# Seven shared PSUM banks and a two-key-tile order in a fused decoder layer on one core

## What is computed

```python
x = x + attn(layernorm(x))            # causal self-attention, 2 heads of 64, rotary positions
x = x + xattn(layernorm(x), ctx)      # 16 heads of 8 over 1601 context rows
x = x + ffn(layernorm(x))             # 128 -> 512 -> 128, erf-GELU, weights with a
                                      # correction taken from 16 of the tokens
# xattn, per batch b and head h:
scores = einsum('bhqd,bhkd->bhqk', Q, K) / sqrt(8)
ctx    = einsum('bhqk,bhkd->bhqd', softmax(scores), V)      # then @ Wo + bo
```

## Time and profile before

| | |
|---|---|
| median of three runs | 377.39 us |
| the profiled execution | 377.22 us |
| its span in the trace | 375.4 us |
| TensorE busy, share of the span | 350.0 us, 93% |
| VectorE busy | 297.1 us, 79% |
| ScalarE busy | 296.4 us, 79% |
| GpSimd busy | 123.5 us, 33% |
| mean granted TensorE clock | 0.986 |

### The profile page before, as it was taken

One profiled execution on the slowest core, in us unless ns is written; L12 is line 12 of the kernel. 1 busy time (PEld: TensorE's weight loads), 2 busy tenths in 40 slices (PEclk: granted clock), 3 DMA queues, 4 the chain that ended last, 5 costly groups with the idle time before them and its releaser, 6 DMA issues.

```text
span 375.4 us, 11889 instructions
## 1 busy us (share of the span) xinstructions
PE 350.0 (93%) x4819; PEld 163.1 (43%) x4819; DVE 297.1 (79%) x601; ACT 296.4 (79%) x598; POOL 123.5 (33%) x202
## 2 busy tenths in 40 slices
PE   7778899999999999999999999999999999999996
PEld 3332343544545444444534445434433434443455
DVE  3779978699998997699999987999977879780013
ACT  1653258989898789898897898898987999799762
POOL 3510746398020205799310133382000036000000
PEclk9999988999999999999999999999998999999999
DMA  7535495033420221135302022023020101000001
GB/s 246 199 107 154 158 274 181 2 135 129 120 84 2 99 95 56 58 131 179 129 27 78 2 79 58 3 63 134 13 69 2 63 19 58 17 2 3 16 2 30
DMA packets 20010, 30.72 MB, mean 82 GB/s; under 512 B 1432, under 2 KB 17218, under 8 KB 19956
## 3 DMA queue, kind: packets, MB, share of 16 engines
q1 hardware_dynamic: 19956, 29.97, 24.8%
HBM read 18.62 MB, written 11.34 MB: 80 GB/s over the span
## 4 chain that ended last, share of the span: by engine, by line
PE 58%; DVE 20%; POOL 10%; ACT 8%; issue 4%; DMA 1%; DVEq 0%; ACTq 0%; POOLq 0%
PE wsum L1191 19%; DVE part_max L785 15%; PE score L1205 13%; PE ring L1161 12%; PE ring L1227 6%; ACT probs L1004 4%; POOL k_parts L630 3%; POOL k_rest L670 2%; POOL k_parts L675 2%; PE score L1161 1%; PE ring L1244 1%; ACT q_unit L1015 1%; PE ring L1252 1%; PE ring L1258 1%; POOL xn L686 1%
## 5 line engine op out<-in xcount | busy, mean ns | idle before, releaser
L785 DVE TENSOR_REDUCE part_max<-ring 128x1 f32<-128x512 f32 x384 | 239.0, 683 | 27.1 <-PE ring L1227 25.3
L1004 ACT ACTIVATE probs<-score 128x512 f32<-128x512 f32 (+1 forms) x416 | 223.3, 597 | 31.3 <-PE score L1205 28.4
L1191 PE MATMUL wsum<-probs,v_aug 128*32 128x256 f32 (+1 forms) x1664 | 134.6, 392 | 3.0 <-ACT unit_ctx L1009 2.9
L1205 PE MATMUL score<-q_unit,k_unit 51*128 51x256 bf16 (+1 forms) x832 | 128.7, 275 | 4.1 <-ACT probs L1004 3.5
L1227 PE MATMUL ring<-k_unit,q_unit 51*128 51x512 bf16 x384 | 121.3, 387 | 3.1 <-DVE part_max L785 2.1
L1205 PEld LDWEIGHTS score<-q_unit,k_unit 51*128 51x128 bf16 (+1 forms) x832 | 48.8, 96 | 97.9 <-ACT probs L1004 57.6
L1191 PEld LDWEIGHTS wsum<-probs,v_aug 128*32 128x32 f32 (+1 forms) x1664 | 39.3, 109 | 39.5 <-issue 20.2
L1227 PEld LDWEIGHTS ring<-k_unit,q_unit 51*128 51x128 bf16 x384 | 35.2, 94 | 17.4 <-DVE part_max L785 9.2
L630 POOL TENSOR_TENSOR max_parts<-neg_max,c_sb 128x8 bf16<-128x8 f32 x16 | 3.4, 210 | 111.9 <-DVE neg_max L793 111.9
L802 DVE RECIPROCAL unit_rsum<-ring 128x8 f32<-128x8 f32 x16 | 3.2, 201 | 21.6 <-PE ring L1252 21.6
L1015 ACT ACTIVATE q_unit<-ring 3x512 bf16<-3x512 bf16 x32 | 18.6, 580 | 1.1 <-PE ring L1244 0.8
(11 more groups left out here) (137 smaller groups left out, 337.8 us busy)
## 6 DMA issues: line engine op xcount, KB each, us to landing
k_unit<-k_rows SPq DMA_DIRECT2D x30, 300.2 KB
ctx_sb<-ctx_t SPq DMA_DIRECT2D x3, 800.5 KB, 8.6
k_rows<-k_parts SPq DMA_DIRECT2D x3, 601.5 KB, 3.2
k_rows<-k_parts SPq DMA_DIRECT2D x3, 599.2 KB, 3.3
even<-ffn_rows SPq DMA_DIRECT2D x3, 512.0 KB, 4.0
q_unit<-q_rows SPq DMA_DIRECT2D x30, 48.0 KB
k_rows<-k_parts SPq DMA_DIRECT2D x3, 401.0 KB, 4.1
k_rows<-k_parts SPq DMA_DIRECT2D x3, 399.5 KB, 3.9
```

Of the source, the lines that this page charges most:

```text
L785: v_.tensor_reduce(part_max[:, par, q, head, hp, c:c + 1], ring[s][:, 0:MW], AX.X, ALU.max)\
L1004: a_.activation(probs[0:rows, i % PB, :], score[k % EB][0:rows, :], ACT.Exp)\
L1191: last = mm(wsum[32 * j:32 * j + 32, 0:S], v_aug[0:rows, v // UB % 3, at:at + 32], probs[0:rows, i % PB, S * (j // 2):S * (j // 2 + 1)], s ...
L1205: last = mm(score[i % EB][0:keys, S * hp:S * (hp + 1)], k_unit[rows, u, L * hp + P * t:L * hp + P * t + keys], q_unit[rows, u, hp, :], sta ...
```

## The change

All seven banks beside `wsum` become one ring (`NR = 7`), which S items and the `HIDDEN` feed-forward steps also take from, in plan order. `wsum` is now where `keep` writes, and the two `keep` ahead of the last `norm` are gone. The `last` item becomes `l0` and `l1`, each with a slot of the ring.

The order inside a unit changes. PV items come in twos, behind every key tile with an odd running number `g = 13 v + t`. Side work of an even `g` (but for `t = 12`) is held and goes behind the odd key tile after it, ahead of that one's own side work. Where the two PV items belong to two units, the first one goes ahead of the side work and the second behind it. `COUNT`, `SIDE`, `TURN_AT` and the `HIDDEN` order stay.

```diff
-EB = 3
-NR = 4
+NR = 7
...
-TAIL = (("keep", 2), ("norm", UNITS - 1), ("keep", 2), ("post", "G0", 2), ("post", "OT", 3), ("keep", 4), ("post", "G1", 2),
+TAIL = (("norm", UNITS - 1), ("keep", 2), ("post", "G0", 2), ("post", "OT", 3), ("keep", 4), ("post", "G1", 2),
...
-        ("post", "last", 3))
+        ("post", "l0", 3), ("post", "l1", 3))
...
 def sums_due(v, t):
     g, h = KT * v + t, KT * HIDDEN_AT[0] + HIDDEN_AT[1]
-    due = range(g - 3, g) if g == h else () if g in (h + 1, h + 2) else range(g - 3, g - 2)
-    return [("PV", *divmod(i, KT)) for i in due if i >= 0]
+    due = range(g - 3, g) if g == h else range(g - 4, g - 2) if g % 2 else ()
+    return [("PV", *divmod(i, KT)) for i in due if i >= 0 and not (g > h > i)]
...
-    plan = []
+    plan, held = [], []
...
         plan += now
+        side = held
         if t == 4 and v:
-            plan.append(("norm", v - 1))
+            side.append(("norm", v - 1))
         if t == TURN_AT[u] and v + 1 < UNITS:
-            plan.append(("mT", v + 1))
+            side.append(("mT", v + 1))
         for *what, off in (SIDE if b < B - 1 else SIDE_LAST).get((u, t), []):
             if 0 <= b + off < B:
-                plan.append((*what, b + off))
+                side.append((*what, b + off))
         if (v, t) in VALUES_AT:
-            plan.append(("prep", VALUES_AT[v, t], 1))
+            side.append(("prep", VALUES_AT[v, t], 1))
         if (v, t) in OUT_AT:
-            plan.append(OUT_AT[v, t])
-        plan += sums
+            side.append(OUT_AT[v, t])
+        held = side if (KT * v + t) % 2 == 0 and t < KT - 1 else []
+        if len({item[1] for item in sums}) == 2:
+            plan.append(sums.pop(0))
+        plan += sums if held else side + sums
...
     for item in PLAN:                                   # ring_slots
-        if item in BANKS or item[0] not in ("M", "mT", "norm", "prep", "post") or item[1] in NO_SLOT:
+        if item[0] == "S":
+            if item[4]:
+                continue
+            item = item[:4]
+        elif item[0] not in ("M", "mT", "norm", "prep", "post") or item[1] in NO_SLOT:
             continue
...
             def exponential(item):
-                i, k = score_index(*item[1:4]), BANKS[item[:4]]
+                i, (s, n) = score_index(*item[1:4]), take(item[:4])
...
-                act.wait_ge(score_filled, k + 1)
-                a_.activation(probs[0:rows, i % PB, :], score[k % EB][0:rows, :], ACT.Exp)\
-                    .then_inc(score_drained, 1)
+                a_.activation(probs[0:rows, i % PB, :], ring[s][0:rows, :], ACT.Exp).then_inc(drained[s], 1)
...
             def keep(n):
-                    mm(score[0][:, :], still[:, 0:P], still[:, :], start=True, stop=True)
+                    mm(wsum[:, :], still[:, 0:P], still[:, :], start=True, stop=True)
...
             def scores(v, t, n, hp, par):
-                if hp == 0 and i >= EB:
-                    pe.wait_ge(score_drained, i - EB + 1)
-                last = mm(score[i % EB][0:keys, S * hp:S * (hp + 1)],
+                if hp == 0 and used:
+                    pe.wait_ge(drained[s], used)
+                last = mm(ring[s][0:keys, S * hp:S * (hp + 1)],
```

More of the change, by code:

```diff
@@ L234, in unit_plan @@
         plan += now
+        side = held
         if t == 4 and v:
-            plan.append(("norm", v - 1))
+            side.append(("norm", v - 1))
         if t == TURN_AT[u] and v + 1 < UNITS:
-            plan.append(("mT", v + 1))
+            side.append(("mT", v + 1))
         for *what, off in (SIDE if b < B - 1 else SIDE_LAST).get((u, t), []):
             if 0 <= b + off < B:
-                plan.append((*what, b + off))
+                side.append((*what, b + off))
         if (v, t) in VALUES_AT:
-            plan.append(("prep", VALUES_AT[v, t], 1))
+            side.append(("prep", VALUES_AT[v, t], 1))
         if (v, t) in OUT_AT:
-            plan.append(OUT_AT[v, t])
-        plan += sums
+            side.append(OUT_AT[v, t])
[3 more added lines that the diff above has]
+        plan += sums if held else side + sums
+    assert not held
     assert not todo
@@ L270 @@
 NO_SLOT = ("ln1", "ln2", "ln3", "soft", "store0", "store1", "split", "pn", "parts0", "parts1", "pa0", "pb0", "pa1", "pb1",
-           "stats", "low", "load", "G0", "G1", "last")
+           "stats", "low", "load", "G0", "G1")
 APART = {("prep", *item[1:]) for item in PLAN if item[0] == "ev"}
@@ L292, in ring_slots @@
     return slots
[L295 to L306, removed]
 RING = ring_slots()
@@ L421, in decoder_kernel @@
         ring = [ctx.enter_context(nc.psum_tensor(f"ring{i}", [P, 512], F32)) for i in range(NR)]
-        score = [ctx.enter_context(nc.psum_tensor(f"score{i}", [P, 512], F32)) for i in range(EB)]
         wsum = ctx.enter_context(nc.psum_tensor("wsum", [P, 512], F32))
@@ L479, in decoder_kernel @@
         low_done = sem("low_done")
-        last_sums = sem("last_sums")
-        last_y = sem("last_y")
         y_free = sem("y_free")
@@ L593, in _ @@
                         .then_inc(even_in, 16)
[L594 to L597, removed]
+                elif kind == "post" and item[1] in ("l0", "l1"):
+                    q = int(item[1][1])
+                    s, n = RING[item]
+                    sp.wait_ge(drained[s], n + 1)
+                    sp.dma_start(out[item[2], P * q:P * (q + 1), :], y_out[:, item[2] % 2, q, :]).then_inc(y_free, 16)
                 elif kind == "post" and item[1] == "out":
@@ L963, in post @@
                     last.then_inc(drained[s], 1)
-                elif name == "last":
+                elif name in ("l0", "l1"):
                     dve.wait_ge(y_free, 16 * (pb // 2 * 2 + 1))
                     dve.wait_ge(x2_b2_set, pb + 1)
[L967 to L970, removed]
+                    s, n = take(item)
+                    q = int(name[1])
+                    v_.tensor_tensor(y_out[:, pb % 2, q, :], ring[s][:, 0:D], x2_b2[:, pb % 3, q, :], ALU.add)\
+                        .then_inc(drained[s], 1)
                 elif name == "out":
@@ L1125, in post @@
                         .then_inc(drained[s], 1)
[L1126 to L1129, removed]
+                elif name in ("h0", "h1") and pb < 2:
+                    s, n = take(item)
+                    gelus(ring[s], pb, int(name[1])).then_inc(drained[s], 1)
                 elif name in ("G0", "G1"):
@@ L1179, in products @@
                 u = v % UB
-                pe.wait_ge(score_drained, BANKS["S", v, t, 1] + 1)
+                s, n = RING["S", v, t, 1]
+                pe.wait_ge(drained[s], n + 1)
                 if t == 0:
@@ L1208, in scores @@
                 if hp == 1:
-                    last.then_inc(score_filled, 1)
+                    last.then_inc(filled[s], 1)
             def maximum(item):
@@ L1385, in post @@
                     pe.wait_ge(low_done, 2 * pb + 1)
[L1386 to L1394, removed]
+                    s = take(item, ("x3T",))
                     for j in (2 * int(name[1]), 2 * int(name[1]) + 1):
-                        last = strips(bank[:, S * (j % 2):S * (j % 2 + 1)], w1_all[:, pb % 2, P * j:P * (j + 1)],
+                        last = strips(ring[s][:, S * (j % 2):S * (j % 2 + 1)], w1_all[:, pb % 2, P * j:P * (j + 1)],
                                       xn3_t[:, pb % 2, :])
-                    last.then_inc(signal, 1)
+                    last.then_inc(filled[s], 1)
                 elif name[0] == "g":
@@ L1405, in post @@
                     pe.wait_ge(low_done, 2 * pb + 2)
[L1406 to L1413, removed]
+                    for needed in ("h0", "h1"):
+                        slot, m = RING["post", needed, pb]
+                        pe.wait_ge(drained[slot], m + 1)
+                    s = take(item)
                     for q in range(QT):
@@ L1418, in post @@
                     last.then_inc(filled[s], 1)
-                elif name == "last":
+                elif name == "l1":
+                    banks = [take(("post", "l0", pb)), take(item)]
                     for j in range(FJ):
@@ L1425, in post @@
                         for q in range(QT):
-                            last = strips(score[1 + q][:, 0:D], hidden[:, pb % 2, j, P * q:P * (q + 1)],
+                            last = strips(ring[banks[q]][:, 0:D], hidden[:, pb % 2, j, P * q:P * (q + 1)],
                                           w2_all[:, pb % 3, D * j:D * (j + 1)], start=j == 0, stop=j == FJ - 1)
                             if j == FJ - 1:
-                                last.then_inc(last_sums, 1)
+                                last.then_inc(filled[banks[q]], 1)
             pe.wait_ge(still_set, 1)
```

9 lines of the change are left out of this document (4 added, 5 removed).

## The result

The changed kernel takes 388.74 us (median of four runs, 387.96 to 391.43) against 377.40 us before: a ratio of 1.031 (95% interval 1.026 to 1.036). It is slower by 11 us where the prediction said 370 us, and outside the predicted range of 360 to 381.

The account below looks back on a forecast made before the run. TensorE was taken to bound the kernel, VectorE and ScalarE close behind. The terms -23 + 6.8 + 4.2 + 3 - 1 + 2 = -8.0 us, shaded to -7.4, took 377.2 to 369.8, given as 370 us; range 360 to 381.

Parts of the forecast that it names:

- What bounds the kernel: Whole kernel: TensorE bounds it at 93% busy, VectorE and ScalarE close behind at 79%, VectorE already full in places.
- the drains: TensorE's changes between scores and weighted sums: 0.09 + 0.14 us saved per pair of key tiles, 100 pairs, -23 us.
- Buffers: Ring of seven banks: half a bank gained for ScalarE, nothing for VectorE; only the start was booked, -1 us.
- seam 1: Between units, the copy of wsum queues behind both tiles' exponentials and TensorE waits: five units x 0.85, +4.2 us.
- VectorE's limit: Pairs with four maxima: 2.4 us of VectorE reductions against TensorE's 1.99, so TensorE waits for banks, +6.8 us.
- Seam 2: A new unit's scores wait for mT's two copies, queued behind exponentials; half hidden by VectorE's backlog, +3 us.
- Bundled side work: Side work held into blocks leaves both evacuating engines unfed longer: +2 us over some twenty blocks.
- The start: At 20 to 62 us, maxima, keys and values get seven banks instead of four: -1 us.
- Rival 3: Seams between units cost more than the drains save, behind ScalarE's queue of exponentials: 382 us, chance 0.19.
- Rival 2: Evacuation bounds the kernel: four maxima take 2.4 us in every pair, TensorE waits for banks everywhere; 377 us, chance 0.12.
- Rival 4: New seam waits of 1.3 us make the granted clock fall to half seven more times: 382 us, chance 0.06.

Follow-up runs that it names:

- lean pair: ring_only and seam_both, each with 174 of 416 maxima left out so nearly every pair has seven bank items at most: 366.9 us and 349.8 us.
- seam_sum: Changed kernel, but an even unit's first weighted sum goes with the next pair, not right behind the previous unit's last: 384.5 us, ratio 1.018.
- seam_both: seam_sum, with mT in odd units also moved from key tile 12 to right behind the scores of key tile 11: 382.3 us, ratio 1.015.
- ring_only: Changed kernel's shared ring of seven banks, with the order of the kernel before: 370.94 us, ratio 0.984.

## Why the prediction was wrong, step by step

- **What bounds the kernel, and the drains: right.** Two sums in a row take 1.00 us (reckoned 1.02), a pair of tiles without a wait 0.97 (0.97). Of the 23 us the part at the sums came, some 12 us with the seams mended (120.5 to 108.2) and 16 in the lean pair. The part ahead of the sums (0.09 per pair) is seen in pairs without a wait, 0.97 against 1.08, but in no kernel's total. The Trainium skill's rule that a change of tiling mode drains TensorE (TensorEngine Tiling, Key Properties) fits these traces: fewer changes, 0.14 us less at each pair of sums and 0.11 ahead of it.
- **Buffers: the step that failed.** It said that in a ring of seven "either blocks the seventh item, about 3.5 scores or maxima", and compared this with the old banks as a depth in backlog. It booked -1 us, nothing for the main phase. It never laid the new burst against the ring: four scores and four maxima are eight. The old order had four items per burst and a pause of 0.58 us for the readers after each. The eighth item waits 1.11 us from the burst's start, which could be had from rows at hand: a score bank filled 0.39 us in (it takes two matmuls; the prediction's seam 1 has it ready at 0.28, after one), an exponential's full length of 0.60, and the hand-overs. 55 pairs of four maxima at 1.43 instead of 0.97 are 25 us, as much as the whole saving; the 17 pairs of five and the 15 of three with side work behind wait too.
- **VectorE's limit (+6.8): the wrong engine.** The pair of 2.4 us that was foreseen from VectorE's rate is nearly what was measured, 2.43, but TensorE waits for ScalarE's exponentials (26.3 and 8.9 us), and so in units where VectorE had room too. VectorE was foreseen near 95% busy over the units; it was busy 243 of 309 us, 79%, where it had been busy 245 of 298.
- **Seam 1 (+4.2): right**, 4 us by seam_sum. **Seam 2 (+3): near in size**, about 2 by seam_both, which the runs do not tell from nothing. Its starting point was misread: the 0.52 us of the earlier trace rows is a wait for a score bank in a unit's last key tile (51*65). The size is near all the same: for `q_unit` itself TensorE's weight loads waited 3.9 us in eight times before and 9.3 in nine in the changed kernel, its matmuls 0.5 and 5.4.
- **Bundled side work (+2)** was priced as hunger of the readers. The runs show another cost: behind three maxima its bank is the eighth item, 1.20 us instead of 0.97, 15 times. The blocks of side work themselves took 54.8 us in all, 53.6 in `ring_only`.
- **The start (-1): right**, the first copy of `wsum` came at 77.6 us instead of 78.6. The last unit took 12.8 us instead of 13.7 from copy to copy, the gain of up to 1 foreseen.
- **Rivals.** Rival 3 had the sign, not the mechanism: the seams were some 6 us. Rival 2 gave a wait for banks at every pair, which is what came, but named VectorE's rate and stopped at no change. The Trainium skill's warning that after tiling the copy out of PSUM may become the bottleneck (TensorEngine Tiling, PSUM Bottleneck) points the right way; here it was the latency of one read, not the rate. Rival 4 is not the cause: the two profiled runs, at granted clocks of 0.987 and 0.986, are 10.9 us apart. But the clock was 0.969 to 0.987 over the four runs of the changed kernel, and the one at 0.969 was the longest, 391.43 us.

In sums: 17 us between the orders at equal banks in the traces (18 in the medians), +19.5 in the blocks of scores and maxima, +1 in side work and -4 at the sums, where some 12 saved are set against some 8 lost at the seams. Less the ring's own gain of 5 to 6 us, that is the 11 us measured.

## What to carry to other kernels

When work is regrouped into longer bursts, count the buffers that one burst takes, side work included, against the buffers that there are. If the burst is longer by even one, its last item waits for the full latency of its first (fill, hand-over, one read, hand-over), even where the reader was idle: here 1.11 us, where its turn was at 0.66. The busy shares of before did not show it. Test a regrouping and a merging of pools apart: here the two edits were worth -6 and +18 us, and only the first was worth keeping.

## What was not expected

The merging of a pool of three and a pool of four banks into one ring of seven, with the order unchanged, gained 1.3 to 1.6% by itself. And taking one of two maxima from a key tile freed no time on TensorE (0.54 us with either): the two halves of the array's rows ran side by side, and in these rows only the longer one counted.
